# Where five of nine expert-weight splits are done in a one-core hybrid layer kernel, and the order of the block they leave

## The reference, cut to what matters

```python
'w_gate': w(ks[2], (E, H, D)), 'w_up': w(ks[3], (E, H, D)), 'w_down': w(ks[4], (E, D, H)),
'ws_gate': w(ks[5], (H, D)), 'ws_up': w(ks[6], (H, D)), 'ws_down': w(ks[7], (D, H))
```

## Time and profile before

| | |
|---|---|
| median of 3 runs | 487.6 us (486.68 to 488.59) |
| the profiled execution, its own time | 487.41 us |
| its span in the trace | 485.6 us |
| granted TensorE clock, mean | 0.996 |
| first block | 0 to about 122.7 us of the span |
| slot 0 of the second block | about 123 to 159 us |

### The profile page before, as it was taken

One profiled execution on the slowest core, in us unless ns is written; L12 is line 12 of the kernel. 1 busy time (PEld: TensorE's weight loads), 2 busy tenths in 40 slices (PEclk: granted clock), 3 DMA queues, 4 the chain that ended last, 5 costly groups with the idle time before them and its releaser, 6 DMA issues.

```text
span 485.6 us, 10621 instructions
## 1 busy us (share of the span) xinstructions
PE 461.7 (95%) x3690; PEld 322.0 (66%) x3690; DVE 393.0 (81%) x1056; ACT 365.2 (75%) x710; POOL 349.0 (72%) x401
## 2 busy tenths in 40 slices
PE   8898999999799999968999989999999999999996
PEld 7675789998466655536665747575657665766664
DVE  6889899788667868998899899979997867486765
ACT  2699999867777757945999669976897588767652
POOL 3673778878556596798788988698969683575652
PEclk9999999999999999998999999999999999999999
DMA  8111100101200000000000000000000000000000
GB/s 265 64 33 34 33 1 3 34 0 36 72 1 2 0 1 1 3 0 1 2 2 1 1 2 1 0 1 3 1 0 24 1 1 24 1 1 1 23 1 24
DMA packets 7061, 8.51 MB, mean 18 GB/s; under 512 B 608, under 2 KB 5216, under 8 KB 7008
## 3 DMA queue, kind: packets, MB, share of 16 engines
q1 hardware_dynamic: 7008, 7.83, 5.1%
HBM read 6.78 MB, written 1.05 MB: 16 GB/s over the span
## 4 chain that ended last, share of the span: by engine, by line
PE 46%; DVE 9%; POOL 8%; ACT 7%; issue 4%; DVEq 0%; ACTq 0%; POOLq 0%
PE bank L1601 8%; PE bank L1602 8%; PE bank L1605 8%; PE bank L1628 5%; PE bank L1630 5%; PE bank L1629 5%; DVE x L2010 2%; POOL b_hid_lo L2253 2%; DVE b_hid L1984 2%; PE bank L1729 1%; PE bank L1746 1%; ACT b_silu L1801 1%; PE bank L1671 1%; PE bank L1635 1%; ACT b_hid_hi L1808 1%
## 5 line engine op out<-in xcount | busy, mean ns | idle before, releaser
L2253 POOL TENSOR_TENSOR b_hid_lo<-b_hid,b_hid_hi 128x512 f16<-128x512 f32 x143 | 169.7, 1195 | 62.8 <-ACT b_hid_hi L1808 60.4
L1984 DVE SCALAR_TENSOR_TENSOR b_hid<-bank,b_silu 128x512 f32<-128x512 f32 x144 | 97.7, 686 | 38.2 <-ACT b_silu L1801 28.6
L1801 ACT ACTIVATE b_silu<-bank 128x512 f32<-128x512 f32 x144 | 85.5, 595 | 43.7 <-PE bank L1605 42.7
L1601 PE MATMUL bank<-x_hi,wsplit 128*128 128x512 f16 x284 | 108.0, 380 | 2.5 <-DVE b_hid L1984 1.7
L1628 PE MATMUL bank<-wsplit,b_hid_hi 128*128 128x128 f16 x576 | 101.2, 220 | 8.3 <-DVE x L2010 4.2
L1602 PE MATMUL bank<-x_hi,wsplit 128*128 128x512 f16 x284 | 107.8, 380 | 0.0
L1605 PE MATMUL bank<-x_lo,wsplit 128*128 128x512 f16 x284 | 107.6, 379 | 0.0
L1630 PE MATMUL bank<-wsplit,b_hid_lo 128*128 128x128 f16 x576 | 101.2, 220 | 0.0
L1629 PE MATMUL bank<-wsplit,b_hid_hi 128*128 128x128 f16 x576 | 101.2, 220 | 0.0
L1808 ACT CAST b_hid_hi<-b_hid 128x512 f16<-128x512 f32 x144 | 88.0, 611 | 13.4 <-DVE b_hid L1984 13.0
L2010 DVE SCALAR_TENSOR_TENSOR x<-bank,b_w_branch,x 128x128 f32<-128x128 f32 x256 | 71.6, 341 | 10.0 <-PE bank L1630 9.6
(11 more groups left out here) (247 smaller groups left out, 926.8 us busy)
## 6 DMA issues: line engine op xcount, KB each, us to landing
moe_raw<-in_moe SPq DMA_DIRECT2D x9, 384.0 KB, 3.2
x<-in_x SPq DMA_DIRECT2D x4, 256.0 KB, 4.3
out<-x SPq DMA_DIRECT2D x3, 256.0 KB, 2.7
rope<-in_rope SPq DMA_DIRECT2D x1, 512.0 KB, 6.0
wzx<-in_wzx SPq DMA_DIRECT2D x1, 386.0 KB, 6.4
b_w_rkvo<-in_w_rkvo SPq DMA_DIRECT2D x1, 256.0 KB, 2.7
b_w_fk<-in_w_fk SPq DMA_DIRECT2D x1, 256.0 KB, 2.9
b_w_fv<-in_w_fv SPq DMA_DIRECT2D x1, 256.0 KB, 3.6
```

The lines of the kernel that those rows point to most:

```text
L1601: nc.tensor.matmul(dst, hi, x_hi[:, q % 2, :], start=True, stop=False)
L1801: nc.scalar.activation(silu[:, 2 * (u % 2) + blk, :], gate_ps[blk][:, :], ACT.Silu, scale=GU_UNSCALE).then_inc(silu_ready, 1)
L1984: nc.vector.scalar_tensor_tensor(hid[:, 2 * (u % 2) + blk, :], up_ps[blk][:, :], GU_UNSCALE * H_SCALE, silu[:, 2 * (u % 2) + blk, :], ALU. ...
L2253: nc.gpsimd.tensor_tensor(hid_lo[:, slot, :], hid[:, 2 * (u % 2) + blk, :], hid_hi[:, slot, :], ALU.subtract).then_inc(lo_ready, 1)
```

## The change

`FRONT_SPLITS = 4`: the first block keeps the loads of branches 0 to 6 and the splits of branches 0 to 3. The splits of branches 4 to 8 are done in units 2 to 6 of the second block: the high part at place 1 of ACT, the low part at place 2 of DVE, each two units ahead of its use. The loads of branches 7 and 8 go behind the four weight loads in the second block's SP queue, each waiting for a split. PE waits for the low part at the start of units 4 to 8. `moe_raw` lives through both blocks. The hand-written lists of PE, ACT, DVE and POOL in the first block are put into another order; apart from the ten split steps they hold the same steps.

```diff
+FRONT_SPLITS = 4
-            for e in range(BRANCHES):
+            for e in range(FRONT_SPLITS + MOE_RING):
                 if e >= MOE_RING:
                     sp.wait_ge(moe_lo, e - MOE_RING + 1)
...
+                if FRONT_SPLITS <= u < BRANCHES and blk == 0:
+                    pe.wait_ge(split_lo, u - FRONT_SPLITS + 1)
...
+            def split_high(e):
+                act.wait_ge(core.moe_w_in[e], 16)
+                nc.scalar.mul(moe_pair(e, 0), moe_raw(e), W_SCALE).then_inc(split_hi, 1)
+
...
+                if q == 0 and FRONT_SPLITS <= e + 2 < BRANCHES and place == 1:
+                    split_high(e + 2)
...
+            def split_low(e):
+                dve.wait_ge(split_hi, e - FRONT_SPLITS + 1)
+                nc.vector.scalar_tensor_tensor(moe_pair(e, 1), moe_raw(e), W_SCALE, moe_pair(e, 0), ALU.mult,
+                                               ALU.subtract).then_inc(split_lo, 1)
+
...
+                if q == 0 and FRONT_SPLITS <= e + 2 < BRANCHES and place == 2:
+                    split_low(e + 2)
...
+            for e in range(FRONT_SPLITS + MOE_RING, BRANCHES):
+                sp.wait_ge(split_lo, e - MOE_RING - FRONT_SPLITS + 1)
+                sp.dma_start(core.moe_raw[:, e % MOE_RING], io["moe"][e]).then_inc(core.moe_w_in[e], 16)
```

The new order, in the places that the prediction speaks of. PE, from the third transposition of `x`:

```diff
+            keep_warm(3)
             project_q(1, 0)
             project_q(1, 1)
             project_q(2, 0)
             project_q(2, 1)
-            keep_warm(5)
...
-            keep_warm(10)
-            turn_x(3)
-            keep_warm(11)
-            keep_warm(12)
-            keep_warm(13)
-            turn_h(0)
...
+            turn_x(3)
+            turn_h(0)
+            project_q(3, 0)
+            project_in(0, 0)
+            project_in(0, 1)
+            keep_warm(4)
+            project_z(0)
+            keep_warm(5)
+            keep_warm(6)
```

Seven more `keep_warm` stand among the projections of the first two sequences, six of them in threes, the last, number 13, before `turn_tok(0)`. ACT:

```diff
             square_q(4)
-            split_high(0)
             square_q(5)
             square_q(6)
+            square_q(7)
             copy_xnT(3)
-            square_q(7)
-            split_high(1)
+            split_high(0)
             copy_hT(0)
-            split_high(2)
```

DVE, around the chain of `adt`:

```diff
             taps(1, 0)
             taps(1, 1)
+            split_low(1)
             add_dt_bias()
             taps(1, 2)
+            finish_dt()
+            split_low(2)
             taps(1, 3)
-            split_low(2)
-            finish_dt()
-            split_low(3)
+            masking(0)
             taps(2, 0)
```

More of the change, by code:

```diff
@@ L761, in _ @@
             closing(13)
-            split_low(6)
-            split_low(7)
-            split_low(8)
+            split_low(3)
             closing(14)
@@ L1007, in _ @@
             copy_gT(13)
-            split_high(8)
             square_g(14)
@@ L1308, in _ @@
             within(3)
+            seg_sums(5)
             turn_tok(8)
-            seg_sums(5)
             turn_g(2)
-            add_state(3)
-            turn_tok(9)
-            seg_sums(6)
-            project_in(3, 3)
-            project_out(2)
-            within(4)
-            products(6)
-            carry(4)
-            turn_tok(10)
-            seg_sums(7)
+            project_in(3, 3)
+            carry(4)
+            seg_sums(6)
+            turn_tok(9)
+            project_out(2)
@@ L1322, in _ @@
+            products(6)
+            seg_sums(7)
+            within(4)
+            turn_tok(10)
+            seg_sums(8)
+            turn_g(3)
+            add_state(3)
             products(7)
             within(5)
+            project_out(3)
             carry(5)
             turn_tok(11)
+            seg_sums(9)
             add_state(4)
-            seg_sums(8)
-            turn_g(3)
+            turn_g(4)
+            turn_tok(12)
             within(6)
             carry(6)
+            project_out(4)
@@ L1331, in _ @@
+            add_state(5)
             products(8)
[L1332 to L1335 removed]
+            turn_tok(13)
             within(7)
[L1337 to L1348 removed]
+            seg_sums(10)
@@ L1349, in _ @@
+            products(9)
+            carry(7)
+            turn_g(5)
+            products(10)
+            seg_sums(11)
+            project_out(5)
+            within(8)
+            turn_g(6)
+            add_state(8)
+            products(11)
             project_out(6)
             within(9)
+            turn_g(7)
             carry(10)
-            add_state(10)
-            turn_g(7)
-            seg_sums(11)
+            add_state(9)
             project_out(7)
+            within(10)
             turn_tok(14)
-            products(10)
+            products(12)
@@ L1358, in _ @@
             seg_sums(12)
             turn_g(8)
-            products(11)
-            within(10)
+            add_state(10)
+            seg_sums(13)
             project_out(8)
-            products(12)
             carry(11)
-            add_state(11)
             turn_tok(15)
             products(13)
-            seg_sums(13)
+            turn_g(9)
+            add_state(11)
             within(11)
+            project_out(9)
+            seg_sums(14)
+            turn_first()
             carry(12)
-            add_state(12)
+            products(14)
@@ L1391, in _ @@
+            carry(14)
+            add_state(13)
             within(14)
             within(15)
+            turn_g(13)
+            carry(15)
             project_out(12)
```

463 lines of the change are left out of this document (219 added, 244 removed).

## The result

The changed kernel takes 489.89 us (median of 17 runs, 488.66 to 491.83); the kernel before, run beside it, 487.28 (17 runs, 486.06 to 488.78). The ratio is 1.005, with a 95% interval of 1.004 to 1.0061: slower by 0.5%, 2.6 us, and the interval leaves no doubt that it is slower. The forecast of 488.3 is 1.6 us short. The prediction drew the line between the same time and slower at 0.5%, or 490.0 us: the ratio lies just over it, the time just under, so on which side of that line it fell is chance. In the profiled execution the span grew from 485.6 to 488.2 us, with the same busy time on PE.

What follows compares the result with a forecast made beforehand. PE was taken to bound the first block after 57 us and slot 0, ACT 20 to 57 us. 487.41: 0 - 0.6 + 1.3 = 488.1, as median 488.3 us; range 485.5 to 491.0.

Steps and rivals of the forecast that it cites:

- Slot 0: Second block's units from 130 to 160 us: receiving the five splits loses 1.3 us, bounds 0 and 4.
- the queues have caught up by unit 6: Slot 0: after one 1.0 us stall at `down(3)`, `add(4)` ends 0.9 us before `down(5)`, so no second stall.
- the 0.3 us for exclusion between DVE and POOL: Slot 0, around unit 4: `split_low` meeting `low` on POOL was taken to cost 0.3 us more.
- The rival of a DVE bound in every unit: Slot 0: each split waits for a full `low` on POOL, 0.7 us in five units; 491.4 us, chance 0.16.
- The front, 57 to 122 us: First block, PE-bound: lighter ACT and DVE remove part of 1.7 us hesitation; 0.6 us gained, bounds 0 and 1.7.
- The front, 20 to 57 us: First block's early part: a 1.0 us lead at the first `project_in` is spent again; 0, doubt 1.5 us either side.
- mostly but not all in waits: Early first block: ten `keep_warm` now after the lead, 2.2 us in all, would fall mostly into PE's waits.
- The end of the front: First block before `closing(14)`: splits were covered by PE's last products, so 0; 0.87 us if that cover were gone.
- The clock: PE at 18 to 20 us: fewer fillers let the granted clock fall, costing 2.6 us; 491 us, chance 0.04.
- The signs that the prediction named for itself: Forecast wrong if barrier moves over 2 us, low splits run well over 1 or `low` over 1.5, or several `down` wait.

Runs made afterwards that it cites:

- experiment 8: Changed kernel with nine `keep_warm` back in their old place, decay exponential in unit 0, and `normalise(3)` ahead of `turn_q(2, 0)` again: 488.06 us, ratio 1.0016.
- 3: Changed kernel with nine `keep_warm` back ahead of the transposes and the decay exponential moved from unit 4 to unit 0: 487.89 us, ratio 1.0008.
- experiment 10: The changed kernel run again, nothing edited, for a second profile: 490.0 us, ratio 1.0056.
- 5: Kernel before with the five splits moved to slot 0, first block's old order kept, and the decay exponential in unit 0: 487.62 us, ratio 1.0004.
- experiment 11: Kernel before with five splits moved, old order kept, decay exponential in unit 0, a statistics step moved from unit 6 to 7: 487.12 us, ratio 0.999.
- Experiment 4: Changed kernel with the first block's four lists in the order of before, less the ten moved split steps: 488.96 us, ratio 1.0035.
- experiment 6: Kernel before with its `keep_warm` steps at the places of the changed kernel, no split moved: 487.76 us, ratio 1.0007.
- experiment 2: Changed kernel with the decay exponential moved from unit 4 to unit 0, removing two table loads: 489.59 us, ratio 1.0044.
- 9: Changed kernel without the eleven fillers `keep_warm(3)` to `keep_warm(13)`: 489.07 us, ratio 1.003.

## Why the prediction was right or wrong

**The account.** From the table, us: rest of the new order 0.13 (experiment 8 less before), `normalise(3)` behind `turn_q(2, 0)` 0.26 (3 less 8), late fillers 0.57 (10 less 3), the wait at `down(3)` 1.18 (changed less 3), `split_low(8)` behind `low` 0.50 (5 less 11). Sum 2.64. The executions at full clock differ by 2.49. The medians differ by 489.89 - 487.28 = 2.61; that this is so near to the sum is in part chance, as the medians of the other experiments show. The fall of the clock near 20 us comes on top in some executions, and the later part of the kernel adds nothing. The sizes rest on one profile of each kernel; the smaller two, 0.13 and 0.26, are near to what such a comparison can tell.

**Slot 0: mechanism right, size nearly.** The forecast had a stall of 1.0 us at `down(3)`, for `add(2)` behind `split_low(6)`, caused by the two table loads. The profile has 1.01 us there, and moving the loads removes 1.18. `hidden(4, 1)` was forecast at 141.95 on the clock of the kernel before; it came at 143.72, and the block had begun 1.77 later, which is 141.95. The forecast said that the queues have caught up by unit 6; there the 0.3 us for exclusion between DVE and POOL came due, as 0.5 us in one place, at `split_low(8)`. The walk left out that a statistics step stands in unit 6. Term 1.3, measured 1.68. No PE wait for a split, and the loads of `moe_raw` cost nothing, as forecast. The rival of a DVE bound in every unit didn't come: four of five splits took 0.95 us.

**The front, 57 to 122 us: the step that failed.** The term was -0.6 us, on the thought that part of 1.7 us of hesitation on PE goes when ACT and DVE get lighter. Experiment 4 takes the work away and keeps the order, and the first block was 0.10 us longer. PE stays busy 64.96 of 65 us. So the spacing of 0.49 against 0.43 us doesn't come from the load on ACT and DVE; what it comes from stays open. The gain was nothing, which is the bound that I had set as the worst case.

**The front, 20 to 57 us: mis-sized.** The term was 0 with 1.5 us of doubt, and it measured 0.96 (118.00 - 117.04, which includes the end). Two assumptions went wrong. "`rms_norm_first` isn't earlier" was taken to mean that it isn't later; it starts 0.57 us later, since DVE waits for POOL's `q`, and takes 0.57 longer. In experiment 10 the first `project_in` comes 16.30 us behind the second statistics against 16.36 before: of the lead of 1.0 us, 0.06 came. And the late fillers "mostly but not all in waits" cost 0.57 us (nine of the ten, by experiments 3 and 10); experiment 6 has 0.45 for them in the old order.

The middle of this stretch differs too. Counted from the second statistics, `adt` starts at 40.44 us before, 39.88 in experiment 10 and 41.29 in the first profile, with its fall of the clock: a lead of 0.56 where the clock held; the forecast had 1.64. The wait of 1.26 us for the logarithm was in the forecast, with 1.4; the wait of 1.27 for `project_dt(3)` was not. DVE had no such wait before; in PE's new list that step stands behind `project_in(1, 3)` instead of ahead of it. `project_in(2, 1)` came 4.65 us later than before in experiment 10 (43.70 against 39.05), forecast 3.5. Little of this reached the barrier: experiment 8 has both, with 1.46 us of wait and `project_in(2, 1)` at 42.87, and ends 0.13 us behind the kernel before. So the forecast was right that scan work fills that place.

**The end of the front: right.** DVE has 1.86 us of idle behind the split.

**The clock.** This rival had 0.04, at 2.6 us. It came in the first profile at 1.4 us and not in the second, nor in that of experiment 2. The place was right; the change is slower without it, by 2.49 us at full clock. The size was read loosely: the earlier trace rows has 5.49 us for the first 24 passes, where the working has 5.28.

**The signs that the prediction named for itself.** All three came in part. The first block grew by over 2 us in the first profile (2.38) but not in the second (0.96). `low` took over 1.5 us beside four splits, at no cost to PE, and one split took 1.97. Two `down` waited, where one was forecast.

**The sum.** 0.96 + 1.68 = 2.64 us against the forecast of 0.7, on a before of 487.3 to 487.6: the forecast missed 0.6 by the gain that wasn't there, 0.96 in the early front, 0.38 in slot 0.

**What the move could give.** With the costs taken away that the runs found (experiment 11: the old order, the early exponential, the late statistics) it is 487.12 against 487.47, a ratio whose interval includes 1. The splits left a place where they cost PE nothing and went to one where at best they cost nothing.

## What to carry to other kernels

Work that lay in the shadow of the bounding engine gave nothing when it was moved; the new place could only cost, so look there for the one unit that has something extra in it (table loads here, a statistics step there) before counting averages. In a list that is kept in order, ask of each pair that is swapped what the new head waits for, and what had been filling that wait. The fillers that keep PE busy were free only where nothing else was ready for it.

## What the runs showed that I had not expected

- Two waits of 0.7 and 0.4 us on PE, between 17.6 and 20.2 us, were followed in one execution by a granted clock of 0.65 and 0.50, down to 1.2 GHz, and in three others with the same two waits (experiments 2, 9 and 10) by 1.00. One profile can't say whether a gap costs the clock.
- All kernels have an idle of 3.4 us on PE that ends between 220 and 224 us. The granted clock behind it differs by execution. The stretch between the first adds of slots 2 and 3 took 48.97 us in the changed kernel's first profile (clock 1.00 in the window from 220 to 224 us), 49.94 in that of before (0.57), and 51.1 in experiment 10 (0.75, then 0.50 in the next 4 us). That is 2 us of scatter with no cause in the change, near to the whole effect. Setting executions of the same mean clock against each other takes it out.
- Whether `split_low(8)` took 0.95 or 1.97 us was open where it came due 1.125 to 1.14 us behind the first of two `low`: once it went first, at 1.125, and in the eight others, from 1.126 up, it came last. Due 0.07 us earlier, it went first each time.
